# Attention and mixture-of-experts kernel: key sums of three heads by additions, as the exponentials come, instead of by one reduction

## The reference

```
x = x + ln2(attention(ln1(layernorm(x))))
x = x + experts(layernorm(x))

# attention: 16 heads of 64, one key head and one value head for all of them
q = xn @ Wq ; k, v = split(xn @ Wkv)
attn = softmax(q_h k^T * 64**-0.5)            # over 512 keys
out  = concat_h(attn @ v) @ Wo
# experts: 8 of them, the 2 best of each token, gate and up 512 wide, gelu(gate) * up, down to 128
```

## Time and profile before

| | us |
|---|---|
| median of 3 runs | 672.04 (670.11 to 673.27) |
| the profiled execution | 670.06 |
| its span in the profile | 668.3 |
| TensorE busy | 582.5 (87%) |
| VectorE busy | 429.6 (64%) |
| GpSimd busy | 381.6 (57%) |
| ScalarE busy | 308.3 (46%) |
| the three reductions of L811 together | 11.1 |

### The profile page before, as it was taken

One profiled execution on the slowest core, in us unless ns is written; L12 is line 12 of the kernel. 1 busy time (PEld: TensorE's weight loads), 2 busy tenths in 40 slices (PEclk: granted clock), 3 DMA queues, 4 the chain that ended last, 5 costly groups with the idle time before them and its releaser, 6 DMA issues. The chain is left out here.

```text
span 668.3 us, 8667 instructions
## 1 busy us (share of the span) xinstructions
PE 582.5 (87%) x2569; PEld 331.9 (50%) x2569; DVE 429.6 (64%) x792; ACT 308.3 (46%) x578; POOL 381.6 (57%) x315
## 2 busy tenths in 40 slices
PE   2799999999999999899999899999550995999990
PEld 1455545445544544455454444443210784888880
DVE  3786568578568786855868685679864372444443
ACT  3245654455464642546554344653125541455540
POOL 4357667576579665976966497872625035333331
PEclk9999999999999996999999799999785698899996
DMA  6111101011011000400000000000127101220005
GB/s 164 64 65 65 66 0 65 15 51 66 0 65 64 1 1 5 143 13 1 1 1 1 5 16 13 1 1 0 33 72 215 32 22 44 73 58 22 23 14 188
DMA packets 27053, 29.29 MB, mean 44 GB/s; under 512 B 4403, under 2 KB 18997, under 8 KB 27008
## 3 DMA queue, kind: packets, MB, share of 16 engines
q1 hardware_dynamic: 24736, 24.50, 11.5%
q0 software_dynamic: 2272, 4.24, 2.0%
HBM read 13.73 MB, written 15.32 MB: 43 GB/s over the span
## 5 line engine op out<-in xcount | busy, mean ns | idle before, releaser
L899 ACT ACTIVATE prob<-s_ps 128x512 f32<-128x512 f32 x256 | 150.8, 598 | 192.1 <-PE s_ps L1008 186.4
L805 DVE TENSOR_REDUCE rowmax<-max_ps 128x1 f32<-128x512 f32 x256 | 173.4, 686 | 90.1 <-PE max_ps L977 87.6
L744 POOL TENSOR_TENSOR fold<-prob 128x1024 f32<-128x1024 f32 x61 | 145.0, 2377 | 102.4 <-ACT prob L899 101.9
L1022 PE MATMUL pv_ps<-prob,v 128*64 128x512 f32 x512 | 140.5, 628 | 0.0
L1006 PE MATMUL s_ps<-q_hl,khh 128*128 128x512 f32 x256 | 118.9, 464 | 0.9 <-ACT prob L899 0.4
L977 PE MATMUL max_ps<-khh,q_hl 128*128 128x512 f32 x256 | 105.8, 422 | 9.1 <-DVE q_hl L794 4.4
L1008 PE MATMUL s_ps<-q_hm,kly 65*128 65x512 f32 x256 | 102.9, 402 | 0.0
L1156 POOL DMA_INDIRECT parts<-eow,xs x39 | 38.2, 981 | 91.8 <-DVE eow L1205 90.9
L1006 PEld LDWEIGHTS s_ps<-q_hl,khh 128*128 128x128 f32 x256 | 49.0, 192 | 80.1 <-ACT prob L899 57.8
L750 POOL TENSOR_TENSOR psums<-fold 128x512 f32<-128x512 f32 x61 | 79.0, 1295 | 4.8
L977 PEld LDWEIGHTS max_ps<-khh,q_hl 128*128 128x128 f32 x256 | 50.6, 198 | 30.0 <-DVE rowmax L805 10.3
(11 more groups left out here) (194 smaller groups left out, 775.4 us busy)
## 6 DMA issues: line engine op xcount, KB each, us to landing
sorted_rows<-blank SPq DMA_DIRECT2D x36, 260.0 KB, 2.6
raw_w<-in_gate_upT SPq DMA_DIRECT2D x7, 512.0 KB, 4.4
xs<-sorted_rows SPq DMA_DIRECT2D x39, 65.0 KB, 1.8
wd<-in_downT SPq DMA_DIRECT2D x8, 256.0 KB, 6.9
xs<-parts SPq DMA_DIRECT2D x8, 256.0 KB, 4.1
x<-in_x SPq DMA_DIRECT2D x4, 256.0 KB, 5.5
out<-x SPq DMA_DIRECT2D x4, 256.0 KB, 2.7
parts<-eow,xs POOLq DMA_INDIRECT x39
```

The lines of the kernel that those rows point to most:

```text
L744: nc.gpsimd.tensor_tensor(fold[:, :, :], prob[:, head % 4, 0:2, :], prob[:, head % 4, 2:4, :], ALU.add).then_inc(prob_folded, 1)
L805: nc.vector.tensor_reduce(rowmax[:, group % 2, it, i:i + 1], max_ps[:, k % 2, :], AX_X, ALU.max).then_inc(max_done, 1)
L899: nc.scalar.activation(prob[:, head % 4, jt, :], s_ps[:, k % 2, :], ACT.Exp, scale=SCALE).then_inc(exp_done, 1)
L1022: last = nc.tensor.matmul(pv_ps[DH * hd:DH * hd + DH, :], v[:, b % 2, jt, :], prob[:, head % 4, jt, :], start=(jt == 0), stop=(jt == JT - 1))
```

## The change

The reduction over the four quarters of `prob`, issued at the last EXP of the head, is replaced by three additions of two 128x512 tiles: at the second EXP of the head quarters 0 and 1 are added to `psums`, at the third and the fourth EXP the next quarter is added to it. Each addition waits for its own EXP alone. The first two are linked (VectorE waits for their end), the third raises `vec_sum`. GpSimd's heads and all other steps stay as they were, and so does the order on the other four engines.

```diff
-                    if kind == "EXP" and a % JT == JT - 1 and vector_sums(u * UH + a // JT):
-                        head = u * UH + a // JT
-                        dve.wait_ge(exp_done, (head + 1) * JT)
-                        dve.wait_ge(sum_mm, (head - SUM_SLOTS) // 4 + 1)
-                        nc.vector.tensor_reduce(psums[:, head % SUM_SLOTS, :],
-                                                prob[:, head % 4, :, :].rearrange("p j s -> p s j"), AX_X,
-                                                ALU.add).then_inc(vec_sum, 1)
+                    if kind == "EXP" and a % JT >= 1 and vector_sums(u * UH + a // JT):
+
+                        head, jt = u * UH + a // JT, a % JT
+                        total = psums[:, head % SUM_SLOTS, :]
+                        if jt == 1:
+                            dve.wait_ge(sum_mm, (head - SUM_SLOTS) // 4 + 1)
+                        dve.wait_ge(exp_done, head * JT + jt + 1)
+                        added = nc.vector.tensor_tensor(total, prob[:, head % 4, 0, :] if jt == 1 else total,
+                                                        prob[:, head % 4, jt, :], ALU.add)
+                        if jt < JT - 1:
+                            link(dve, added)
+                        else:
+                            added.then_inc(vec_sum, 1)
```

## The result

The changed kernel took 663.65 us (median of 6 runs, 663.05 to 665.49), the kernel before 670.43 in the same runs (its three runs of the first table and three more, 669.57 to 673.27). The ratio is 0.9894, 95% interval 0.9871 to 0.9916: 1.1% faster, 7 us, between 5.6 and 8.6. I had forecast 667.5, within 664.8 to 670.8, so the direction was right and the size too small. Timed once more, on another occasion, it gave 0.9916 (0.9888 to 0.9944), 5.6 us. The profiled execution took 665.49 us, the slowest of its six, with a span of 663.8.

A forecast was written before the change was run, and what follows sets the result against it. The end of the attention was taken to bound the kernel, with TensorE waiting on VectorE's reduction. Terms 0.5 + 2.95 + 1.1 = 4.55 us, off the 672.04 us median, gave 667.5 us, range 664.8 to 670.8.

The forecast's parts named there:

- The bound and the place of the gain: End of the attention: a microsecond won before 494.38 us is won at the end; TensorE's two late waits hang on VectorE.
- Head 59: Its additions: first held by GpSimd's fold, CHOOSE0 0.5 us earlier, which counts for nothing because TensorE is busy.
- Head 61: Two additions ahead of the `ao` of NORM 6,3 delay SUM 7,0 by 1.0 us, hidden by a later wait.
- my lower case: Delay of SUM 7,0 of 0.7 us if L455 starts ahead of the fold and the first addition waits for EXP 21.
- its cover: TensorE's 3.68 us wait before NORM 7,0, at 473.45 us, said to hide the delay of SUM 7,0.
- The path to `rhl`: VectorE before NORM 7,0: L501 escapes the fold of head 62, `rih` is held instead; 0.5 us won, the most uncertain term.
- Head 63: Only one addition follows EXP 31, so SUM 7,1 starts at T + 5.9 instead of T + 8.85: 2.95 us won.
- nothing moves: Early additions delay the `ao` of NORM 7,0 to T + 2.9, but NORM 7,1 already ran at T + 3.0.
- Behind SUM 7,1: TensorE at full clock after a pause shrunk to some 0.4 us; 1.1 us won up to NORM 7,2.
- clean passage: Rival: `rih` gets ahead of the fold of head 62; 5.95 us won, 666.1 us, chance 0.15.
- The rivals: Four other outcomes: 670.1 us (chance 0.22), 666.1 (0.15), 672 (0.07) and 682 (0.06); the forecast itself had 0.50.
- another core or an unknown queue: Second block, 550.92 to 565.85 us: unexplained ScalarE and VectorE waits; a rival had them as long again, 682 us, chance 0.06.

The follow-up runs named there:

- together61: The changed kernel with head 61's three additions all issued at its last exponential, behind the `ao` of NORM 6,3; ratio to the kernel before 0.9939.
- all_together: The changed kernel with the three additions of each of heads 59, 61 and 63 all issued at that head's last exponential; ratio to the kernel before 0.9941.
- after_again: The changed kernel without any edit, timed and traced once more; ratio to the kernel before 0.9916.
- before_fold_late: The kernel before, reductions kept, with GpSimd's fold of head 62 made to wait for `rhl` of RSPLIT 7,0; ratio to the kernel before 0.9997.
- fold_late: The changed kernel with GpSimd's fold of head 62 made to wait for `rhl` of RSPLIT 7,0; ratio to the kernel before 0.9975.
- only59_61: The changed kernel with additions for heads 59 and 61 only, head 63 keeping its one reduction; ratio to the kernel before 0.9934.
- extra_add: The changed kernel with three more unread additions on VectorE behind EXP 31, ahead of head 63's third addition; ratio to the kernel before 0.9967.
- together61_busy: The changed kernel with head 61's additions issued at its last exponential, plus 17 unread TensorE products in the last unit's pauses; ratio to the kernel before 0.9925.

## Why the prediction was right or wrong

- **The bound and the place of the gain: right.** The whole gain that two traces agree on, 5.9 us, lies between `rhl` of RSPLIT 6 and the second block, and the chain from there on is unchanged but for scatter.
- **Head 59: the holding right, "counts for nothing" wrong.** Its additions took 2.80 and 1.65 us (I had 2.9 and 1.6); the `ao` ended 1.3 us ahead of NORM 6,1, as I had it. But the 0.5 us by which CHOOSE0 comes earlier (0.63 measured) does reach TensorE, through ScalarE's exponential of the router: SUM 7,0 comes 0.38 us earlier by it (together61 against before). When these additions are issued doesn't matter: all_together reaches SUM 7,0 with together61 (16.83 and 16.85).
- **Head 61: the delay of SUM 7,0 was mis-sized.** "I take 1.0", between 0.7 and 1.3; it was 0.35 (17.58 - 17.23). That is 0.73 by head 61's two early additions (after_again against together61), which is my lower case, less the 0.38 of head 59. L455 did get in ahead of the fold, and when EXP 21 let the first addition begin, at 457.14, it took 0.69 us. And the pause before NORM 7,0 is not "its cover", as I wrote: the fold of head 62 is tied to TensorE (468.53 - 443.16 = 25.37 behind e, before 25.02), and through it `rih`, `rhl` and T. My own sum had it so, my sentence on the cover not; together61 shows 0.75 us of T for 0.73 of SUM 7,0.
- **The path to `rhl`: right in mechanism.** L501 took 0.23, `rih` 2.25 and `rhl` 1.63, and T came 4.3 us behind the fold's start, as in my sum. With the fold 0.65 us earlier than I had it, because SUM 7,0 was delayed by 0.35 and not by 1.0, the term is 1.2 instead of 0.5 us. before_fold_late and fold_late show the cause by taking the fold away.
- **Head 63: the step "nothing moves" failed.** I left the first low stretch of the clock as it is, because "the pause ahead of it is still 2 us". The clock stayed at 1.00 behind 2.09 us. PV 12 took 1.08 us instead of 1.98, and from NORM 7,1 to the end of the last scores it took 0.93 instead of 1.45, so EXP 31 was done at T + 4.5 (476.73 + 0.60 - 472.84), not 5.1. The early additions moved something too: alone, the full clock brings EXP 31 to T + 3.76 (only59_61), and the additions ahead of the `ao` put it back by 0.73. Nor did the third addition follow EXP 31 at once; it began 0.19 later, behind the `ao` of NORM 7,1. The term is 3.4 us instead of 2.95.
- **Behind SUM 7,1: right.** 1.24 us for my 1.1, at full clock. But my reason, the shorter pause, was too simple: only59_61 kept the full clock there behind the same 3.38 us pause.
- **The sum.** 1.2 + 3.4 + 1.2 = 5.9 us instead of 4.55. Of the 3.85 us between 667.5 and 663.65, that is 1.3. Another 1.6 is the base: I started from the median of three runs, 672.04, and six gave 670.43. The remaining 0.9 is what the first medians show beyond 5.9; the second timing gave 5.6 by its ratio, so I take it for scatter. So three things made the forecast too high: the base (1.6), the term of the path to `rhl` (0.7) and that of head 63 (0.45). VectorE's busy time fell by 5.4 us (429.6 to 424.2), not by 4. The lower end of my range allowed 1.3 us for the scatter of the runs, below the clean passage; the base alone was off by 1.6.
- **The rivals.** None came. The clean passage has the number, 5.95 us against 5.9, but by luck: `rih` did not get ahead of the fold (2.25 us). The waits for "another core or an unknown queue" were as long as before (3.43 us the first, 5.82 the last, in a stretch of 14.92 us, before 14.94); what they are stays open, and no run was made for it.

The rule of the Trainium skill (page "SBUF — State Buffer", section "Who interferes with whom"), that a VectorE instruction with two SBUF inputs contends with a GpSimd instruction that reads SBUF, held in this trace: 2.80 us for an addition of 0.69 that began 0.12 us behind GpSimd's fold. Of the nine additions only the first two of head 59 were hit, and even so its key sum was done 0.63 us earlier against e than with the reduction.

## What to carry to other kernels

Count what stands behind the last input of the last stage, but price what you move ahead of it as well. Three additions of 0.69 us in place of a reduction of 3.6 won 1.9 us where they stood; moving two of them forward won only 0.15 more, since they then stood in VectorE's queue ahead of results that the last input itself waited for. A delay on an engine that is waiting later is covered only if that later wait ends on something that the delay doesn't move too. And where runs scatter by a few microseconds, cut the trace at two points that frame the change: the stretch between them repeated to 0.04 us where the gain by the medians went from 6.8 to 6.2 us.

## What the runs showed of the hardware

- Executions that run the same code up to a point reach it up to 4.7 us apart (440.85 to 445.54).
- Whether the clock falls doesn't follow from the pause just ahead. Behind a pause of 3.38 us it was low in the kernel before and full in only59_61; behind 2.41 us it was full in extra_add, and then low at the last OUT. In together61 it fell there although the longest pause of the last unit ahead of it was 2.06 us. In seven variants it fell at the last OUT (3.02 to 3.33 us instead of 2.07), and 0.9 to 1.5 us of the gain went back; unread products in the pauses kept it up in together61_busy. What decides it stays open.
- A VectorE instruction on 128x64 elements, 0.22 us alone, took 2.36 us when it met a GpSimd addition of 2.37 us (before_fold_late).
- Adding four quarters of 128x512 in one reduction took 3.62 to 3.82 us, in three additions 2.1 us.
